# Projection by 512-token units, unit products on GpSimd, and a later slope reload in the closing part of an attention-and-experts kernel

## What is computed

```python
xn = layernorm(x)
q, k, v = heads(xn @ wq.T + bq), heads(xn @ wk.T + bk), heads(xn @ wv.T + bv)   # 16 heads of 16
off = tanh(pw_w @ gelu(depthwise_conv3(q)) + pw_b) * 6.0                      # 12 offsets for each head and token
pos = clip(arange(q) + linspace(-2, 2, 12) + off, 0, q - 1)
sk, sv = linear_interpolation(k, pos), linear_interpolation(v, pos)
attn = softmax(q . sk / 4 - rel_scale * abs(pos - arange(q)))                 # over the 12 samples
s = (sum attn * sv) @ wo.T + bo
g = silu(top2_of_8_experts(xn))                                             # gated expert layers, 256 -> 512 -> 256
out = x + s * g
```

## Time and profile before

| | us |
|---|---|
| median of three runs (1502.31 to 1509.05) | 1505.02 |
| the profiled execution, whole | 1504.18 |
| its span, first to last instruction | 1502.5 |
| TensorE busy | 1371.1 (91%) |
| VectorE busy | 1292.2 (86%) |
| ScalarE busy | 823.2 (55%) |
| GpSimd busy | 782.2 (52%) |

### The profile page before, as it was taken

How to read it: one execution, slowest core, us unless ns; L and a number is a source line. 1 busy time by engine, 2 the same in 40 slices (tenths; PEclk the granted TensorE clock), 3 DMA queues, 4 the chain that set the end, 5 groups by cost and what they waited for, 6 DMA issues and landing times.

```text
span 1502.5 us, 35981 instructions
## 1 busy us (share of the span) xinstructions
PE 1371.1 (91%) x13751; PEld 1092.3 (73%) x13752; DVE 1292.2 (86%) x1544; ACT 823.2 (55%) x1889; POOL 782.2 (52%) x536
## 2 busy tenths in 40 slices
PE   5998999994799999999999999999999878798887
PEld 4864565564688888888888887888888756576666
DVE  7837756665799999999999999999999999989971
ACT  2547677675355555555555445545454436565555
POOL 1001477630677867868676767778676642211011
PEclk9998999996899999999999999999999978898899
DMA  7943455555957676757677666668667679999898
GB/s 227 329 153 89 129 182 183 181 199 165 288 148 216 184 231 159 232 139 232 184 212 213 169 179 169 191 161 248 179 173 217 148 156 224 252 206 250 222 237 158
DMA packets 202457, 293.50 MB, mean 195 GB/s; under 512 B 23809, under 2 KB 159237, under 8 KB 202099
## 3 DMA queue, kind: packets, MB, share of 16 engines
q0 software_dynamic: 64768, 146.57, 38.4%
q1 hardware_dynamic: 134915, 144.84, 32.9%
q10 hardware_dynamic: 2672, 0.83, 0.2%
HBM read 182.83 MB, written 117.73 MB: 200 GB/s over the span
## 4 chain that ended last, share of the span: by engine, by line
DVE 50%; PE 8%; issue 7%; DMA 6%; SPq 3%; ACT 1%; POOL 0%; POOLq 0%; DVEq 0%; ACTq 0%
DVE gslope L1689 12%; DVE parts L1685 12%; DVE parts L1645 8%; DMA band<-band_rows 5%; DVE expert_mem L1611 5%; PE pB L1522 3%; DVE parts L1657 2%; DVE parts L1661 2%; DVE parts L1664 1%; PE pY L1532 1%; PE pA L1507 1%; DVE gslope L1742 1%; DVE wgt L1750 1%; SPq L1163 1%; PE pBT L1507 1%
## 5 line engine op out<-in xcount | busy, mean ns | idle before, releaser
L1217 POOL DMA_INDIRECT moe_rows<-expert_mem,token_of x142 | 342.7, 2413 | 78.5 <-issue 44.5
L1198 POOL DMA_INDIRECT expert_mem<-xn_rows,token_of x142 | 210.2, 1480 | 139.4 <-issue 90.3
L1488 PE MATMUL pA<-xsT,expert_mem 128*128 128x256 f32 x1136 | 263.8, 386 | 15.3 <-DMA expert_mem<-in_w_l 11.4
L1494 PE MATMUL pY<-expert_mem 128*128 x1136 | 267.0, 388 | 0.0
L1488 PE MATMUL pB<-xsT,expert_mem 128*128 128x256 f32 x1136 | 256.8, 379 | 0.0
L1488 PEld LDWEIGHTS pA<-xsT,expert_mem 128*128 128x128 f32 x1136 | 219.1, 194 | 49.9 <-issue 10.4
L1494 PEld LDWEIGHTS pY<-expert_mem 128*128 128x128 f32 x1136 | 212.0, 191 | 42.8 <-issue 16.3
L1488 PEld LDWEIGHTS pB<-xsT,expert_mem 128*128 128x128 f32 x1136 | 215.8, 190 | 29.3
L1685 DVE SCALAR_TENSOR_TENSOR parts<-pos_pair,prob 128x768 f32<-128x768 f32 x256 | 227.9, 952 | 1.1
L1689 DVE TENSOR_REDUCE gslope<-parts 128x256 f32<-128x3072 f32 x64 | 214.7, 3354 | 2.2
L1339 ACT ACTIVATE expert_mem<-pA,b1sel 128x256 f32<-128x256 f32 x284 | 111.4, 475 | 154.5 <-DVE expert_mem L1611 65.7
(11 more groups left out here) (207 smaller groups left out, 2069.9 us busy)
## 6 DMA issues: line engine op xcount, KB each, us to landing
expert_mem<-in_w_l POOLq DMA_DIRECT2D x71, 1024.0 KB, 6.8
band<-band_rows SPq DMA_DIRECT2D x256, 96.0 KB, 5.2
S_rows<-stage SPq DMA_DIRECT2D x64, 376.0 KB, 2.5
band_rows<-wgt SPq DMA_DIRECT2D x12, 1536.0 KB, 7.0
pos_pair<-pos_rows SPq DMA_DIRECT2D x28, 384.0 KB, 8.0
xn_rows<-stage SPq DMA_DIRECT2D x16, 512.0 KB, 5.7
v_rows<-stage SPq DMA_DIRECT2D x16, 512.0 KB, 4.3
moe_rows<-zeros POOLq DMA_DIRECT2D x4, 2048.0 KB
```

Of the source, the lines that this page charges most:

```text
L1198: nc.gpsimd.indirect_dma_start(out=xs[:, u, s], out_offset=None, in_=dram["xn"], in_offset=bass.IndirectOffsetOnAxis(ap=keep["inv"][:, 2 * ...
L1217: nc.gpsimd.indirect_dma_start(out=dram["moe"], out_offset=bass.IndirectOffsetOnAxis(ap=keep["inv"][:, 2 * n + s:2 * n + s + 1], axis=0), ...
L1488: mm = nc.tensor.matmul(dst[:, c], w1[:, 1 - u, k, o * HID + c * P:o * HID + (c + 1) * P], xsT[:, k], start=(k == 0), stop=(k == KC - 1))
L1494: mm = nc.tensor.matmul(pY[:, s], hid[:, h, c, s * P:(s + 1) * P], w2[:, c, ds(e * D, D)], start=False, stop=(s == 1 and c == HC - 1))
```

## The change

1. `project` handles half a unit at once: two tiles' worth of rows, one bias matmul over 512 columns and eight weight-and-moving passes, into a whole PSUM bank. It runs one unit late, behind tiles 0 and 2 of the next unit. The last unit still goes tile by tile. `outT` holds whole units, and its columns are read with a step of four, so that partition p gets tokens 4p to 4p + 3.
2. A unit's rows of `out` and `moe_rows` are therefore moved as runs of four rows (4 KB for a partition) and not four separate rows of 1 KB.
3. ScalarE copies 128x512 out of PSUM at once.
4. The 15 unit products move from VectorE (`UNITS_AT`) to GpSimd's queue, ahead of each `store_unit`, and `UNITS_BY` says how many are done before each store of weights. `proj` has 8 slots, no longer 10.
5. SP reloads step 14's slopes behind the loads of tiles 4 and 5, no longer ahead of them.
6. The exponentials stand behind tiles 0, 14, 27 and 40, and `prepare` behind tiles 8 and 21.

```diff
-ROW_SLOTS = 10
+ROW_SLOTS = 8
-END_EXPONENT_AT = (0, 14, 28, 42)
-END_PREPARE_AT = (6, 21)
+END_EXPONENT_AT = (0, 14, 27, 40)
+END_PREPARE_AT = (8, 21)
-UNITS_AT = ({}, {5: 1, 7: 1}, {1: 1, 3: 1, 5: 1, 7: 1}, {1: 1, 3: 1, 6: 1}, {4: 1, 6: 1})
+UNITS_BY = (1, 4, 7, 10)
...
         def unit_rows(t, k):
-            return t[k * GTOK:(k + 1) * GTOK, :].rearrange("(a p) c -> p a c", p=P)
+            rows = t[k * GTOK:(k + 1) * GTOK, :]
+            return rows.rearrange("(p a) c -> p a c", a=GROUP) if k < LAST else rows.rearrange("(a p) c -> p a c", p=P)
...
             load_pos(BY_SP)
+            for n in range(BAND_SLOTS, BAND_SLOTS + 2):
+                tile_in(n)
             reload_slope(BY_SP + 2)
-            for n in range(BAND_SLOTS, TILES):
+            for n in range(BAND_SLOTS + 2, TILES):
                 tile_in(n)
...
+            def finish_unit(k):
+
+                pool.wait_ge(pj_ready, 2 * k + 2)
+                pool.wait_ge(moe_ready, k + 1)
+                pool.sem_inc(go, 1)
+                nc.gpsimd.tensor_tensor(proj[:, k % ROW_SLOTS], proj[:, k % ROW_SLOTS], moe[:, k % MOE_SLOTS], ALU.mult).then_inc(
+                    out_ready, 1)
+
             def store_unit(k):
+                finish_unit(k)
                 pool.wait_ge(out_ready, k + 1)
...
+                for k in range(unit, UNITS_BY[it - BY_SP]):
+                    store_unit(k)
+                    load_moe(k + MOE_AHEAD)
+                unit = UNITS_BY[it - BY_SP]
                 store_weights(it)
...
-            def project(t, u):
-                pe.wait_ge(outT_ready, t + 1)
...
+            def project(i, h, u):
+
+                pe.wait_ge(outT_ready, GROUP * i + GROUP)
+                if not (isinstance(i, int) and i == 0):
+                    pe.wait_ge(pj_ready, 2 * i + h - 1)
+                nc.tensor.matmul(pJ[h][:], ones3[:], bo[:, None, :].broadcast_to([NB, 2, D]), start=True, stop=False)
+                for s in range(2):
+                    for c in range(KC):
+                        mm = nc.tensor.matmul(pJ[h][:, s], outT[:, u, c].rearrange("p (q a) -> p a q", a=GROUP)[:, 2 * h + s],
+                                              wo[:, c], start=False, stop=(s == 1 and c == KC - 1))
+                mm.then_inc(pj_done, 1)
...
-            def finish_unit(k):
-
-                dve.wait_ge(pj_ready, (k + 1) * GROUP)
-                dve.wait_ge(moe_ready, k + 1)
-                V.tensor_tensor(proj[:, k % ROW_SLOTS], proj[:, k % ROW_SLOTS], moe[:, k % MOE_SLOTS], ALU.mult).then_inc(out_ready, 1)
```

More of the change, by code:

```diff
@@ L1592, in four_tiles @@
                     times_v(t, j, i)
-                    if not (first and j == 0):
-                        project(t - 1, (j + 1) % 2)
-            four_tiles(0, first=True)
-            with pe.Fori(1, TILES // GROUP - 1) as i:
-                four_tiles(i)
-            four_tiles(TILES // GROUP - 1, last=True)
-            project(TILES - 1, 1)
+                    if not first and not last and j % 2 == 0:
+                        project(i - 1, j // 2, 1 - u)
+                    if last and j < 2:
+                        project(i - 1, j, 1 - u)
+                    if last and j >= 2:
+                        for k in range(t - 2 if j == 2 else t - 1, t if j == 2 else t + 1):
+                            project_tile(k)
+            four_tiles(0, 0, first=True)
+            for i in range(1, 3):
+                four_tiles(i, i % 2)
+            with pe.Fori(1, TILES // GROUP // 2 - 1) as i:
+                for u in range(2):
+                    four_tiles(i * 2 + u + 1, 1 - u)
+            four_tiles(LAST, LAST % 2, last=True)
         @block.vector
@@ L1762, in _ @@
             gate_hidden(1, 1)
-            gated, unit = 2, 0
+            gated = 2
             for it in range(STEPS):
-                gates, units = {}, {}
+                gates = {}
                 for place in GATES_AT[it] if it < len(GATES_AT) else ():
@@ L1768, in _ @@
                     gated += 1
-                for place, some in UNITS_AT[max(it - BY_SP + 1, 0)].items():
-                    units[PLACES[place]] = range(unit, unit + some)
-                    unit += some
-                step(it, it * CHAIN, gates=gates, units=units, first=it == 0, last=it == LAST)
+                step(it, it * CHAIN, gates=gates, first=it == 0, last=it == LAST)
             assert gated == SLOT_PAIRS
-            for k in range(unit, LAST):
-                finish_unit(k)
             for t in range(LAST * GROUP, TILES):
```

86 lines of the change are left out of this document (47 added, 39 removed).

## The result

The changed kernel took 1522.54 us in the median of 4 runs (1519.28 to 1523.86), the kernel before beside it 1503.66 (1498.59 to 1509.05). The ratio is 1.0122 with an interval of 1.0081 to 1.0162: slower, outside the range of 1489 to 1513 that was given. The profiled execution took 1523.68, its span 1521.9, against 1504.18 and 1502.5.

What follows compares the result with a forecast made beforehand. Prediction: VectorE's subtraction of step 15 gates TensorE through ScalarE's exponential. 1397.5 + C (8) + 2.1 + 78.8 of TensorE work + W (6) + 7.2 + 1.7 gave 1501 us, range 1489 to 1513.

Steps and rivals of the forecast that it cites:

- The sum: End time as step 15's subtraction on VectorE, plus 2.1, TensorE's work from there, 7.2 and 1.7: 1501 us.
- C: Time GpSimd's seven products before step 15's subtraction cost VectorE: 8 us taken, half the full hold, bounds 0 and 25.
- rival B: VectorE is held for every GpSimd product, in a row behind a store of weights: 16.8 us, 1510 us; chance 0.18.
- the gate sets the end: ScalarE's exponential waits for VectorE's subtraction of step 15 and holds TensorE, so an earlier subtraction ends the kernel earlier.
- the last gate binds as long as C is above about 2: TensorE would reach tile 42 at 1401.7, before step 15's exponential lets it pass at 1407.6, with stalls ahead kept at 12.2 us.
- The sign that I had given for a wrong form of the sum: TensorE reaching tile 42 only after the gate had opened, for instance because strided weights or late projection slow each tile.
- VectorE's saving: Nine unit products removed before step 15's subtraction, 10.3 us, and waits for ScalarE, 7.9 us: 18.2 us in all.
- W: TensorE's stalls behind the last gate, including lower clock after waits: 6 us taken against 9.5 before, bounds 2 and 14.
- Rival C: Bursts of transfers starve the tiles behind the gate: stalls of 14 us, time 1509 us; chance 0.12.
- The projection "costs the same": On TensorE, eight passes of half a unit equal the passes of two tiles; strided reading of weights put at zero.
- The reload: Moving the slope reload wins perhaps 5 us by tile 8, hidden by the gates behind tiles 14, 27 and 40.
- The tail: From TensorE's end to the span's end 7.2 us, with unit 14's GpSimd product covered, else costing up to 2 us.

Runs made afterwards that it cites:

- e4: Changed kernel with GpSimd's products of units 0 to 10 each timed to begin with one of VectorE's one-input reductions: 1518.72 us, ratio 1.0087 to the kernel before.
- e3: Changed kernel without its 15 unit products (output incomplete), stores and loads kept: 1546.06 us, ratio 1.0283 to the kernel before.
- e12: Changed kernel with the closing part's exponentials and preparations back at their old places: 1521.95 us, ratio 1.0107 to the kernel before.
- e8: Kernel before with unit products on GpSimd, units 0 to 10 timed to VectorE's reductions; old projection and 1 KB rows: 1506.1 us, ratio 1.0015.
- e10: e8 with the late half-unit projection added, plus its copies of 128x512 and eight slots: 1516.26 us, ratio 1.0062 to the kernel before.
- e9: Changed kernel with the projection spread evenly, a quarter behind each tile: 1519.63 us, ratio 1.0094 to the kernel before.
- e11: e10 with the even pace, each half's eight passes split over two tiles: 1509.43 us, ratio 1.0029 to the kernel before.
- e5: Changed kernel with rows of 1 KB and contiguous weights instead of 4 KB runs and strided weights: 1516.69 us, ratio 1.0084 to the kernel before.
- e7: Kernel before with only the slope reload moved behind the loads of tiles 4 and 5: 1501.26 us, ratio 0.9995.
- e15: e3 with each unit's store at its old instant and only the load held half a unit: ratio 1.0085 to the kernel before.
- e14: e3 with each unit's store and load both held until one more half unit is copied: ratio 1.0246 to the kernel before.
- e18: e16 with eleven loads of expert rows put at places of their own in VectorE's step: 1606.27 us against 1618.94, ratio 0.9922 to the kernel before.
- e16: e8 with the slope reload of e7 added: ratio 1.0001 to the kernel before.
- e17: e4 with loads of expert rows put at places of their own in VectorE's step: ratio 1.0046 to the kernel before.

## Why the prediction was wrong, step by step

**The sum.** Term by term on the profiled execution: the subtraction ended at 1414.5 where I had 1405.5 (+9.0). Tile 42 followed 2.0 us later, as said. Then 94.8 us to TensorE's end (1511.33) where I had 78.8 + 6 (+10.0). The tail took 10.6, not 7.2 (+3.4). That is the 22.4 us between 1501.3 and 1523.7.

**C, mis-sized: 8 for some 16.** VectorE's stretched instructions add up to 15.6 us, and 1414.5 less the 1397.5 that I had without them is 17.0. I took half the full hold because the nearest row showed GpSimd giving way. The stretched rows above show both: GpSimd gives way while VectorE issues back to back, then VectorE is held 2.0 to 2.8 us at the next instruction. The product's own length was right (2.4 taken, 2.38 measured), and rival B's form of it, products in a row behind the store of weights, is what the trace shows, with the subtraction at 1414. The Trainium skill, page SBUF — State Buffer, section "Who interferes with whom", has the lock and that reductions are free of it, and this case agrees: 2424 ns a product in the mean of e4, 3882 in the changed kernel. That the waiting side may be GpSimd for a whole run of VectorE's instructions, 13.27 us for a product of 2.38, is what these rows add. The 4497 ns that the prediction takes from the Trainium skill's page GPSIMD Engine Reference, section 3.1, stand there for an addition; the estimate of 2.25 us made from them lies 6% below the 2.38 us measured for a product.

**That the gate sets the end: the step that failed.** I argued that removing work ahead of the gate moves the end by as much. e4 moves the gate by 10 us and the end by 4 to 5, with overlapping intervals; e3 moves it by 10.6 us, and the end comes 24 us later; e12 takes the wait at the gate away for nothing; and in e8 the gate opens 19.0 us earlier, and TensorE is at tile 44 no sooner. I had TensorE at tile 42 by 1401.7 if no gate held it. In the changed kernel it is there at 1412.95 (the 3.56 us of waiting end at 1416.51), and in e4, without a gate in its way, at 1418.39: it is late by itself. My claim "the last gate binds as long as C is above about 2" rested on stalls ahead of the gate staying at 12.2 us, and nothing in the profile warranted that. The gate does bind in the changed kernel, by 3.56 us, but it is not what sets the end: with it out of the way TensorE waits for the tiles' loads. The sign that I had given for a wrong form of the sum, TensorE at tile 42 after the gate has opened, is what e4 shows. What was right is VectorE's saving: 18.2 us by my count, 16.5 in e8, whose subtractions of steps 12 and 15 lie 183.2 us apart and not 199.7.

**W, mis-sized: 6 for some 16, outside my bounds of 2 to 14.** The waits behind the gate are 11.6 us by the view above; of the rest, low clock behind waits is what the rows show (3.80 us at 1471.44 instead of 2.25). Rival C had this mechanism, and at 12% I gave it too little. I took the DMA share of 0.99 as a sign of danger and then priced only the bytes. What counts more is when they leave: 4.1 us of all 16 engines for a store by the earlier trace rows, with a load 0.6 us behind it, against slots for four tiles.

**The projection "costs the same".** Without stalls it does: half a unit's passes take 2.25 us, two tiles' 2 x 1.13. The strided weights' loads take 329 ns in the mean instead of 203 to 212 before, beside matmuls of 405 ns each at the full clock, and no wait of TensorE for them shows. But it comes a unit late, and e10 puts the whole rearrangement at about 7 us over e8. How much of that is the uneven pace (e9 and e11 take 4 and 5 us off by their ratios, with overlapping intervals) and how much the lateness stays open.

**The 4 KB runs** do need less DMA time, and bring nothing: e5, without them, is if anything faster, by some 5 us. Some 3 of these stand in the tail; the mechanism stays open. **The reload** is worth nothing, as said (e7). **The tail**, mis-sized: 7.2 for 10.6. Unit 14's product was covered, as said: its data came 7.4 us before TensorE's end, and the last store leaves 1.5 us behind TensorE as before. Of the 3.4 us 3.0 lie behind the last bytes, 6.0 us without any work where there were 3.0, and they come with the 4 KB runs (10.6 against 7.8 us in e5). My sum had no term for that, and its cause stays open.

**Together**: VectorE's lock is shown, and the gate as what sets the end is refuted. That the instant of issue costs time is shown on one chip by e15 against e14 (1.6%), and by e18 against e16 (0.8%, across chips, with intervals apart); e17 against e4 (0.4%) lies within the intervals. That lumps make up the changed kernel's 1.2% is not shown. The kernel before sends pairs of store and load too, one at 1259.72 and 1260.51 for instance, but its pairs are 15 to 25 us apart, where those of the changed kernel stand 4 to 9 us apart behind a store of weights. And e17 still lies 0.5% above before, about where e10's late projection is.

## What to carry to other kernels

When TensorE's loads and bulk transfers share DMA engines at a share near 1, price a change by when it issues its bytes, and not only by how many: a store and a load that leave together can cost more than an engine's whole saved work, and giving eight loads places of their own in a queue's idle stretch gave 0.8% here. An in-order gate that one sees binding in a trace is worth moving only as far as the next limit, and what tells of that limit is the view of waits with the DMA share beside it. Put two-input products of GpSimd next to VectorE's reductions.

## What the runs showed of the hardware that I had not expected

A GpSimd product of 128x1024 that takes 2.38 us alone took 13.27 us beside twelve back-to-back two-input instructions of VectorE, which themselves were not slowed (10.52 us for the twelve), and then held the next one for 2.0 us. A kernel with less work, e3, ran some 1.6% longer than the changed kernel that it was cut from (1.0283 against 1.0122). And with equal idle time, 61 us, TensorE's busy time for the same work differed by 19 us between e14 and e15, which the granted clock accounts for: 249.24 us at 0.80 and 230.24 us at 0.87 are both 200 us of full clock. Last, the kernels with 4 KB runs end with 6 us, and those with 1 KB runs with 3 us, in which neither an engine nor a DMA does anything.
